# Keys instead of queries projected, narrow matmuls placed side by side in the array, and the attention ordered pair by pair

## The chip, the cores and the metric

The kernel runs on one core of a Trainium2 chip, alone, in one launch. The metric is the device time of the launch in microseconds (us), the median of several executions. Inside a launch five engines work from their own queues, strictly in the order in which the program lists their instructions: PE (TensorE, matrix products into the eight PSUM banks), DVE (VectorE), ACT (ScalarE), POOL (GpSimd) and SP, which here only issues DMAs. They wait for each other through semaphores.

## The reference

The input is 32 batches of 64 tokens with 128 features, so 2048 tokens in all. Each batch attends to its own 64 context tokens with 8 heads. Then comes a layer norm, a small feed-forward net (FFN) of width 256, a second layer norm, and a mixture of experts: two shared experts that every token uses and 16 routed ones, of which each token uses four, chosen by a router.

```python
def attention_block(query, ctx):              # query = layernorm(x), (32, 64, 128)
    q = einsum('bsd,hdk->bhsk', query, Wq)    # 8 heads of 128
    k = einsum('btd,hdk->bhtk', ctx, Wk)
    v = einsum('btd,hdv->bhtv', ctx, Wv)
    A = softmax(m * (q @ k^T) + (1 - m) * -1e30)
    proj = concat_heads(A @ v) @ Wo
    x1 = layernorm(ctx + proj) * gamma[0] + beta[0]
    ffn = relu(x1 @ W1 + b1) @ W2 + b2
    return layernorm(x1 + ffn) * gamma[1] + beta[1]
x = x + attention_block(layernorm(x), ctx)
h = layernorm(x)
scores = sigmoid(h @ router_w.T)              # 2 of 4 groups, then 4 of 16 experts
y = sum over experts e of combine[t, e] * ((silu(h @ gate[e]) * (h @ up[e])) @ down[e])
out = x + y + shared experts
```

## The kernel before

**Tiling.** The 2048 tokens are 16 tiles of 128 (`NT`). A tile is a pair of batches of 64 tokens. Four pairs make a chunk of 512 tokens (`CH = 4`, `TPC = 4`, `CW = 512`). A pair is written (c, p) for chunk and place before, and m = 0 to 15 after.

**Preparation.** On load the weights of a head are folded: PE transposes Wq, Wk and Wv (L1201, 24 transposes), multiplies Wq Wk^T (L1208) and Wv Wo (L1218), and ACT and DVE split each result in a high and a low part of type fp32r (`fold_high`, `fold_low`).

**Attention, by chunk.** PE transposes the normalised x and the context (`turn_xn`, `turn_ctx`). `queries` makes for every head the folded query of the whole chunk, as three fp32r matmuls of 512 columns (L1059 to L1061), and ACT copies each out of PSUM (L501). For a pair, `scores` runs eight fp32 matmuls of 128 columns (L1122); in each, half the result belongs to the other batch of the pair and is thrown away. `values` makes context times folded Wv Wo, six fp32r matmuls, and ACT copies them out (L510). The softmax of a pair goes over four engines: DVE adds the mask (L768, two instructions) and takes the maximum (L774), POOL subtracts it (L348), ACT takes the exponential (L516), DVE sums and inverts (L780, L783), POOL scales (L357). PE transposes the result (L1132), ACT spreads it into a block-diagonal tile (L525, two copies), `attend` runs eight fp32 matmuls of 128 columns over the heads into one bank (L1144), and DVE adds the context (L788).

**After attention, by chunk, one or two chunks behind:** layer norms (`statistics` and `normalise` on DVE, the inverse root on POOL as L338 or L343, L340), the FFN on PE (`turn_x1` L1159, `ffn_up` L1164, `ffn_down` L1171; `hidden` L535 on ACT), the turned and split input of the experts (`turn_xm` L1183, `xm_high`, `mT_low`) and the router's logits (`route`). The routing itself is about 40 small DVE instructions for eight tiles at a time (`bias_scores`, `group_scores`, `keep_groups`, `keep_experts`, `combine`).

**Experts.** A step k is one expert on one chunk: `up` (six fp32r matmuls, L1059 to L1061), silu on ACT (L646), the product on DVE (`gate_up`, L988 or L992), the routing weight (`weigh`, on POOL L447 in the first 16 steps, on DVE L1004 later), and `down` (one fp32 matmul of 512 columns, L1331). Before `up(0, k)` may write its second bank, `gate_up` of step k - 2 must be done. There are 72 steps. The first 16 are interleaved by hand with what is left of attention, FFN and routing of the last chunk; from step 16 on it is a steady loop.

**What sets the order** is on every engine an explicit list, in the loops `for c in range(CH + 1)` and in the hand-written sequences behind them (PE from L1334, DVE from L1008, ACT from L671, POOL from L456). PSUM is eight banks: three work banks in rotation, two for scores, and one each for transposed probabilities, attention result and FFN.

## Time and profile before

| what | value |
|---|---|
| median of three runs | 341.67 us (341.66 to 342.0) |
| profiled execution, its own time | 341.1 us |
| its span in the trace | 339.4 us |
| PE busy | 314.8 us, 93% |
| DVE busy | 220.9 us, 65% |
| ACT busy | 145.5 us, 43% |
| POOL busy | 92.0 us, 27% |
| attention, first query matmul to last attend | 15.4 to 152.1 us |
| first expert steps among the rest of the last chunk | 148.7 to 191 us |
| steady expert loop and output | 191 to 339.4 us |

The span is what the trace covers, 1.7 us less than the profiled execution's own time. Busy time of PE is summed over instructions whose ends are modelled, so the distance from the start of one instruction to the start of the next is the better price of one, and such distances are used below. An instruction marked x16 stands for sixteen that are merged in one row; every fp32 matmul is two PE instructions, and an fp32r matmul or a transpose is one.

### The profile page before, as it was taken

What the parts mean: (1) busy time and instruction counts of PE and PEld (TensorE: products, weight loads), DVE (VectorE), ACT (ScalarE), POOL (GpSimd) and SP (SyncE); (2) the same over time, 40 slices, a digit from 0 to 9 for tenths busy, and PEclk for the clock granted to TensorE, in tenths of its full rate; (3) what the DMA queues carried; (4) which work ended last, traced back from release to release, by engine and by line L of the source; (5) the groups of instructions that cost most, each with busy time, mean ns of one, the idle gap of its engine ahead of it and who ended that gap; (6) DMA issues with size and microseconds to landing.
All of it is one profiled execution on the core that took longest, in us unless ns stands there. A gap on an engine that the chain in (4) does not pass through costs nothing.

```text
span 339.4 us, 5140 instructions
## 1 busy us (share of the span) xinstructions
PE 314.8 (93%) x1611; PEld 240.6 (71%) x1611; DVE 220.9 (65%) x568; ACT 145.5 (43%) x266; POOL 92.0 (27%) x105
## 2 busy tenths in 40 slices
PE   3989899999999998986977999999999999999993
PEld 3979789788978896874655666666666666666662
DVE  2818526948895789798676835566566656565654
ACT  2664673477347734662325342333333233333320
POOL 3006413634473444453263042000000000000000
PEclk9999999999999999999997999999999999999999
DMA  8996000000000000002100046333233333323004
GB/s 243 349 272 214 3 0 3 0 0 2 1 3 0 2 0 2 0 4 74 57 0 1 2 138 240 124 116 106 95 118 124 124 124 124 122 114 102 32 0 124
DMA packets 18773, 26.79 MB, mean 79 GB/s; under 512 B 1330, under 2 KB 13124, under 8 KB 18628
## 3 DMA queue, kind: packets, MB, share of 16 engines
q1 hardware_dynamic: 16676, 25.52, 22.8%
q10 hardware_dynamic: 2080, 1.05, 1.1%
q8 instruction: 10, 0.16, 0.2%
q14 instruction: 7, 0.06, 0.0%
HBM read 25.38 MB, written 1.18 MB: 78 GB/s over the span
## 4 chain that ended last, share of the span: by engine, by line
PE 76%; DVE 12%; ACT 4%; issue 3%; POOL 2%; DMA 1%; DVEq 0%; POOLq 0%; ACTq 0%
PE bank L1331 17%; PE bank L1059 12%; PE bank L1061 12%; PE bank L1060 12%; PE bank L1144 8%; PE bank L1122 7%; DVE cen L725 3%; PE bank L1171 2%; DVE sc_m L768 2%; ACT prob_T L525 2%; PE bank L1201 1%; DMA wqk_in<-in_L_xattn_Wq 1%; ACT v_o L510 1%; DVE stat L709 1%; ACT hid L535 1%
## 5 line engine op out<-in xcount | busy, mean ns | idle before, releaser
L646 ACT ACTIVATE wT<-bank 128x512 f32<-128x512 f32 x72 | 43.0, 597 | 84.9 <-PE bank L1061 84.8
L1059 PE MATMUL bank<-mT_hi,we_hi 128*128 128x512 f32 x128 | 74.0, 578 | 3.9 <-DVE wT L992 2.0
L992 DVE TENSOR_TENSOR wT<-bank,wT 128x512 f32<-128x512 f32 x64 | 44.1, 691 | 39.5 <-PE bank L1061 29.8
L1061 PE MATMUL bank<-mT_hi,we_lo 128*128 128x512 f32 x128 | 50.5, 394 | 0.0
L1060 PE MATMUL bank<-mT_lo,we_hi 128*128 128x512 f32 x128 | 50.3, 393 | 0.0
L1059 PEld LDWEIGHTS bank<-mT_hi,we_hi 128*128 128x128 f32 x128 | 24.0, 188 | 22.0 <-issue 12.3
L398 POOL TENSOR_TENSOR we_lo<-w_exp,we_hi 128x256 fp32r<-128x256 f32 x16 | 11.8, 740 | 97.8 <-ACT we_hi L567 97.8
L1331 PE MATMUL bank<-wT,we_dn 128*128 128x512 f32 x72 | 37.5, 605 | 0.0
L1331 PE MATMUL bank<-q_T,we_dn 128*128 128x512 f32 x72 | 36.5, 592 | 0.0
L1060 PEld LDWEIGHTS bank<-mT_lo,we_hi 128*128 128x128 f32 x128 | 24.1, 188 | 16.7 <-issue 14.0
L1122 PEld LDWEIGHTS bank<-cT_m,q_T 128*128 128x128 f32 x256 | 30.3, 192 | 6.4 <-DVE sc_m L768 5.9
L1122 PE MATMUL bank<-cT_m,q_T 128*128 128x128 f32 x256 | 31.6, 276 | 3.2 <-DVE sc_m L768 3.2
L1144 PE MATMUL bank<-v_o,prob_T 128*128 128x128 f32 x256 | 31.9, 278 | 2.1 <-ACT prob_T L525 1.8
L1144 PEld LDWEIGHTS bank<-v_o,prob_T 128*128 128x128 f32 x256 | 30.1, 192 | 4.8 <-ACT prob_T L525 4.6
L1061 PEld LDWEIGHTS bank<-mT_hi,we_lo 128*128 128x128 f32 x128 | 24.0, 188 | 5.4
L348 POOL TENSOR_TENSOR sc_m<-sc_m,nmax 128x512 f32<-128x512 f32 x16 | 16.7, 1043 | 30.8 <-DVE nmax L774 30.8
L510 ACT COPY v_o<-bank 128x512 f32<-128x512 f32 x32 | 17.7, 588 | 15.9 <-PE bank L1144 9.1
L357 POOL TENSOR_TENSOR prob<-sc_m,rsum 128x512 f32<-128x512 f32 x16 | 16.7, 1043 | 25.9 <-DVE rsum L783 25.9
L525 ACT COPY prob_T<-bank 64x512 f32<-64x512 f32 x32 | 18.6, 580 | 7.7 <-PE bank L1132 7.5
L501 ACT COPY q_T<-bank 128x512 f32<-128x512 f32 x32 | 18.2, 589 | 7.7 <-PE bank L1061 5.9
L768 DVE TENSOR_TENSOR sc_m<-bank,mask_add 128x256 f32<-128x256 f32 x32 | 12.0, 416 | 10.3 <-PE bank L1122 10.3
L1331 PEld LDWEIGHTS bank<-q_T,we_dn 128*128 128x128 f32 x72 | 13.7, 190 | 4.3 <-issue 1.4
(181 smaller groups left out, 529.9 us busy)
## 6 DMA issues: line engine op xcount, KB each, us to landing
wvo_in<-comb_dram SPq DMA_DIRECT2D x16, 512.0 KB, 3.5
wqk_in<-comb_dram SPq DMA_DIRECT2D x15, 512.0 KB, 3.6
mask_row<-in_mask_BxS_ff SPq DMA_DIRECT2D x1, 1024.0 KB, 8.8
out_x<-ctx_all SPq DMA_DIRECT2D x4, 256.0 KB, 2.8
x_all<-in_x SPq DMA_DIRECT2D x1, 768.0 KB, 8.2
ctx_all<-in_ctx SPq DMA_DIRECT2D x1, 768.0 KB, 10.5
wqk_in<-in_L_xattn_Wq ACTq DMA_DIRECT2D x1, 512.0 KB, 4.8
wqk_in<-in_L_xattn_Wk ACTq DMA_DIRECT2D x1, 512.0 KB, 5.6
```

The lines of the kernel that those rows point to most:

```text
L501: a.copy(q_T[:, :, h, :], work[k % 3][:].rearrange("p (b s) -> p b s", s=SEQ)).then_inc(work_free[k % 3], 1)
L510: a.copy(v_o[p % 2][:, j * HP:(j + 1) * HP, :].rearrange("p h d -> p (h d)"), work[k % 3][:]).then_inc(work_free[k % 3], 1)
L525: last = a.copy(prob_T[p % 2][rows, :, s, :], t_bank[rows, :].rearrange("p (h s) -> p h s", s=SEQ))
L646: a.activation(silu[k % 2], h_bank[k % 2][:], ACT.Silu).then_inc(silu_ready, 1)
L768: last = v.tensor_tensor(sc_m[i][:, s], sc_bank[s][:].rearrange("p (h t) -> p h t", t=P)[:, :, 0:SEQ], mask_add[:, (2 * p + s) * SEQ:(2 * ...
L992: v.tensor_tensor(s_u[k % 2], u_bank[k % 2][:], silu[k % 2], ALU.mult).then_inc(s_u_ready, 1)
L1059: pe.matmul(dst, w_hi, m_hi, start=start, stop=False)
L1060: pe.matmul(dst, w_hi, m_lo, start=False, stop=False)
L1061: return pe.matmul(dst, w_lo, m_hi, start=False, stop=stop)
L1122: last = pe.matmul(sc_bank[s][:, hp * P:(hp + 1) * P], q_T[:, b, 2 * hp:2 * hp + 2, :].rearrange("p h s -> p (h s)"), cT_m[:, b * SEQ:b * ...
L1144: last = pe.matmul(av_bank[:, 0:P], prob_T[p % 2][:, h, :, :].rearrange("p b s -> p (b s)"), v_o[p % 2][:, h, :], start=(h == 0), stop=(h ...
L1331: pe.matmul(acc[c][:], we_dn[i][:], act[k % 4], start=start, stop=stop).then_inc(down_full, 1)
```

## The change

It rewrites the attention part, and the order of all that stands beside it.

- **Preparation.** The host lays out all weights and inputs as the kernel wants them (`layout`). Wq and Wk come transposed, so the 24 transposes fall away; the fold gives per head a matrix for keys. Only that one is split in high and low; the folded Wv Wo stays one fp32 tile `vo`. Loads are fewer and contiguous. A second copy of the context with its two halves swapped, `ctx_swap`, is loaded as well (1 MB), and the mask is brought in a form for pairs.
- **Keys projected.** `key(c, h)` takes the place of `queries`: the (masked) context of a chunk times the folded weight, three fp32r matmuls per head, copied out by ACT. It runs one chunk ahead: two heads per pair. The odd heads use the scores' bank.
- **Scores in column tiles.** A pair's scores are two fp32 matmuls of 512 columns with a stationary operand of 64 columns: one batch writes partitions 0 to 63 of the bank, the other 64 to 127. The mask is one DVE instruction.
- **Raw context attended in row tiles.** `values` is gone. `attend` multiplies the probabilities (one ACT copy in place of two) with the unprojected context: four fp32 matmuls of 256 columns whose contraction has 64 rows, in the upper or the lower half of the array, into two banks. `heads_out` copies both to SBUF on ACT, and `project` applies `vo`: eight fp32 matmuls of 128 columns.
- **Order.** One loop over m = 0 to 17 on every engine. Scores of pair m, and transposing, attending and projecting of pair m - 2, stand in one turn of it.
- **Beside it.** The layer norms 1 and 3 are applied by ACT in place of DVE (POOL makes one more small product for it). The routing of the first eight tiles stands behind the loop, among the first expert steps, in place of inside the last chunk. In the sequence behind the loop, `add_ctx` of the last pair follows `keep_groups(0)`, and `gate_up(0, 5)` follows `residual(3)` and `statistics(3, 3)`.

The core of the diff. PE:

```diff
-                    for hp in range(HP):
-                        last = pe.matmul(sc_bank[s][:, hp * P:(hp + 1) * P],
-                                         q_T[:, b, 2 * hp:2 * hp + 2, :].rearrange("p h s -> p (h s)"),
-                                         cT_m[:, b * SEQ:b * SEQ + P], start=True, stop=True)
+                    tok = n * P + s * SEQ
+                    pe.matmul(sc_bank[s * SEQ:(s + 1) * SEQ, :], xnT[:, tok:tok + SEQ],
+                              k_T[c % 2][:, b, :, :].rearrange("p h t -> p (h t)"), start=True, stop=True
+                              ).then_inc(sc_full, 1)
...
+            def attend(n):
+
+                pe.wait_ge(prob_T_ready, n + 1)
...
+                for s in range(2):
+                    for j in range(2):
+                        rows = slice(j * SEQ, (j + 1) * SEQ)
+                        held = ctx_all if s == j else ctx_swap
+                        last = pe.matmul(o_bank[j][:].rearrange("p (h b s) -> p h b s", b=2, s=SEQ)[:, :, s, :],
+                                         held[rows, n, :], prob_T[n % 2][rows, :, s, :], start=True, stop=True)
+                        if s == 1:
+                            last.then_inc(o_full[j], 1)
+
+            def project(n):
+
                 for j in range(2):
...
+                    pe.wait_ge(o_taken[j], n + 1)
...
                 for h in range(NH):
...
+                    last = pe.matmul(av_bank[:, 0:P], o_T[n % 2][:, h % 2, h // 2, :], vo[:, h, :],
+                                     start=(h == 0), stop=(h == NH - 1))
...
+            for m in range(NT + 2):
+                c, p = divmod(m, TPC)
+                ahead = c + 1 < CH
+                if m < NT:
+                    scores(m)
+                if ahead:
+                    key(c + 1, 2 * p)
+                if m >= 2:
+                    turn_probs(m - 2)
...
+                if p == 0 and c >= 2:
+                    ffn_up(c - 2, 1)
+                if p == 0 and c >= 3:
+                    turn_xm(c - 3)
+                if p == 1 and c >= 2:
+                    ffn_down(c - 2)
...
+                if m >= 2:
+                    attend(m - 2)
+                if ahead:
+                    key(c + 1, 2 * p + 1)
...
+                if p == 3 and c + 2 < CH:
+                    turn_ctx(c + 2)
+                if p == 3 and c >= 1:
+                    ffn_up(c - 1, 0)
+                if m == NT + 1:
+                    pe.wait_ge(sc_taken, NT)
+                    up(0, 0)
+                if m >= 2:
+                    project(m - 2)
```

ACT:

```diff
+                if ahead:
+                    key(c + 1, 2 * p)
+                if m >= 2:
+                    spread(m - 2)
...
+                if p == 0 and c >= 2:
+                    hidden(c - 2, 1)
+                if p == 0 and c >= 3:
+                    xm_high(c - 3)
...
+                if m < NT:
+                    exponent(m)
+                if m >= 2:
+                    heads_out(m - 2)
+                if ahead:
+                    key(c + 1, 2 * p + 1)
+                if m == NT:
                     router_sigmoid(0)
```

DVE:

```diff
+            for m in range(NT + 1):
+                c, p = divmod(m, TPC)
+                if m >= 3:
+                    add_ctx(m - 3)
+                if m >= 1:
+                    sum_of_exp(m - 1)
+                if m < NT:
+                    mask_and_max(m)
+                if c == 0 and p + 1 < CH:
+                    if p == 0:
+                        v.wait_ge(ld_x, 16)
+                    statistics(0, p + 1, tokens(x_all, p + 1))
+                    normalise(0, p + 1, tokens(x_all, p + 1))
+                if m == 0:
+                    cT_low(1)
...
+            add_ctx(NT - 2)
+            bias_scores(0)
+            group_scores(0)
+            add_ffn(CH - 2)
+            statistics(2, CH - 2, z)
+            keep_groups(0)
             gate_up(0, 0)
...
+            add_ctx(NT - 1)
+            v.wait_ge(y_ready, NT)
+            statistics(1, CH - 1, tokens(y, CH - 1))
+            residual(CH - 2)
             gate_up(0, 1)
+            keep_experts(0)
             statistics(3, CH - 2, tokens(x2, CH - 2))
             gate_up(0, 2)
...
+            combine(0)
             gate_up(0, 3)
+            take_combine(0)
             add_ffn(CH - 1)
             statistics(2, CH - 1, z)
             gate_up(0, 4)
-            gate_up(0, 5)
             residual(CH - 1)
             statistics(3, CH - 1, tokens(x2, CH - 1))
+            gate_up(0, 5)
```

POOL, the opening, the loop and the sequence behind it:

```diff
+            mask_context(0)
             inverse_root(0, 0)
...
+            mask_context(1)
+            pool.wait_ge(ld_mask, 32)
+            pool.tensor_scalar(mask_add[:], mask_add[:], -1.0, BIG, ALU.add, ALU.mult).then_inc(mask_done, 1)
...
+            for m in range(NT + 1):
+                c, p = divmod(m, TPC)
+                if m >= 1:
+                    normalise_probs(m - 1)
+                if m < NT:
+                    subtract_max(m)
+                if c == 0 and p + 1 < CH:
+                    inverse_root(0, p + 1)
...
+            inverse_root(2, CH - 1)
             weigh(4)
-            inverse_root(2, CH - 1)
             weigh(5)
             mT_low(CH - 2)
             inverse_root(3, CH - 1)
```

## Rows read from the trace of the kernel before

**Rows 1.** The page: PE busy in 40 slices, and the clock granted to it.

```profile
PE   3989899999999998986977999999999999999993
PEclk9999999999999999999997999999999999999999
```

**Rows 2.** Timeline, PE, opening: start us, us, engine, line, operation, out<-in, merged count.

```profile
5.71 3.65 PE L1201 MATMUL bank<-ident,wqk_in 128*128 128x128 f32 x16 [5.71 <-DMA wqk_in<-in_L_xattn_Wq]
16.23 0.39 PE L1059 MATMUL bank<-xnT_hi,qk_hi 128*128 128x512 f32 x1
16.91 0.39 PE L1059 MATMUL bank<-xnT_hi,qk_hi 128*128 128x512 f32 x1
22.36 1.95 PE L1122 MATMUL bank<-cT_m,q_T 128*128 128x128 f32 x16
```

**Rows 3.** Timeline, PE, one pair: scores, attend, four transposes, and what follows.

```profile
32.03 1.95 PE L1122 MATMUL bank<-cT_m,q_T 128*128 128x128 f32 x16
33.82 1.95 PE L1144 MATMUL bank<-v_o,prob_T 128*128 128x128 f32 x16
35.61 0.60 PE L1132 MATMUL bank<-ident,prob 128*128 128x128 f32 x4
35.96 0.48 PE L1059 MATMUL bank<-vo_hi,cT_hi 128*128 128x512 f32 x1
```

**Rows 4.** Timeline, PE: scores of the first pair of chunks 1 and 3.

```profile
52.05 1.95 PE L1122 MATMUL bank<-cT_m,q_T 128*128 128x128 f32 x16
120.34 1.95 PE L1122 MATMUL bank<-cT_m,q_T 128*128 128x128 f32 x16
```

**Rows 5.** DMA issues: size and us from issue to landing.

```profile
wvo_in<-in_L_xattn_Wo SPq DMA_DIRECT2D x1, 512.0 KB, 7.2
ctx_all<-in_ctx SPq DMA_DIRECT2D x1, 768.0 KB, 10.5
```

**Rows 6.** Timeline: the softmax of the first pair through DVE, POOL and ACT.

```profile
24.34 0.76 DVE L768 TENSOR_TENSOR sc_m<-bank,mask_add 128x256 f32<-128x256 f32 x2 [7.04 <-PE bank L1122]
25.96 1.04 POOL L348 TENSOR_TENSOR sc_m<-sc_m,nmax 128x512 f32<-128x512 f32 x1 [5.81 <-DVE nmax L774]
27.04 0.63 ACT L516 ACTIVATE sc_m<-sc_m 128x512 f32<-128x512 f32 x1 [3.90 <-POOL sc_m L348]
28.63 0.68 DVE L780 TENSOR_REDUCE esum<-sc_m 128x8 f32<-128x512 f32 x1
29.46 0.83 DVE L709 BATCH_NORM_STATS2 stat<-x_all 128x6 f32<-128x128 f32 x4
```

**Rows 7.** Timeline, ACT in chunk 3: an exponential, the next instruction, a pair of copies.

```profile
129.00 0.63 ACT L516 ACTIVATE sc_m<-sc_m 128x512 f32<-128x512 f32 x1 [0.20 <-POOL sc_m L348]
129.54 0.29 ACT L561 ACTIVATE wqk_in<-logits 128x128 f32<-128x128 f32 x1
143.65 1.07 ACT L510 COPY v_o<-bank 128x512 f32<-128x512 f32 x2 [1.49 <-PE bank L1144]
```

**Rows 8.** Timeline: an fp32 matmul of 512 columns, and its reader's start.

```profile
160.68 1.02 PE L1164 MATMUL bank<-x_T,w_in 128*128 128x512 f32 x2
161.74 0.69 ACT L535 ACTIVATE hid<-bank,small_T 128x512 f32<-128x512 f32 x1 [0.96 <-PE bank L1164]
```

**Rows 9.** Windows with the routing's tile alone on DVE: busy us and count.

```profile
129.80:150.80 21.00, 9.22 (x43) 1.00 0.01 2
```

**Rows 10.** Timeline behind the attention: from the last pair to expert step 9.

```profile
153.85 0.29 DVE L788 TENSOR_TENSOR ctx_all<-bank,ctx_all 128x128 f32<-128x128 f32 x1
166.81 0.69 DVE L793 TENSOR_TENSOR x_b<-bank,x_b 128x512 f32<-128x512 f32 x1 [2.27 <-PE bank L1171]
169.71 1.29 POOL L447 TENSOR_TENSOR wT<-wT,wqk_in 128x512 f32<-128x512 f32 x1 [6.62 <-DVE wT L992]
181.07 1.09 PE L1183 MATMUL bank<-ident,cen 128*128 128x128 f32 x4 [1.72 <-DVE cen L725]
184.72 0.47 PE L1059 MATMUL bank<-mT_hi,we_hi 128*128 128x512 f32 x1
```

More of the change, by code:

```diff
@@ L518, in spread @@
-            def spread(c, p):
-                a.wait_ge(t_full, c * TPC + (p + 1))
-                if not (c == 0 and p < 2):
-                    a.wait_ge(av_full, c * TPC + (p - 1))
-                for s in range(2):
-                    rows = slice(s * SEQ, (s + 1) * SEQ)
-                    last = a.copy(prob_T[p % 2][rows, :, s, :],
-                                  t_bank[rows, :].rearrange("p (h s) -> p h s", s=SEQ))
-                last.then_inc(prob_T_ready, 1)
+                    for h in range(NH - 2, NH):
+                        a.wait_ge(key_full[h % 2], key_use(c - 1, h))
@@ L913, in take_combine @@
                 v.tensor_copy(comb_T[0:rows, b, :], comb_bank[b][0:rows, 0:P]).then_inc(comb_T_ready, 1)
-            for c in range(CH + 1):
-                now, last, before = c < CH, c >= 1, c >= 2
-                if last:
-                    sum_of_exp(c - 1, 3)
-                if before:
+            for m in range(NT + 1):
[14 more added lines that the diff above has]
+                if p == 0 and c >= 3:
+                    mT_low(c - 3)
+                    take_logits(c - 3)
+                if p == 1 and c >= 2:
@@ L921, in _ @@
                     add_ffn(c - 2)
[L922 to L925 removed]
                     statistics(2, c - 2, z)
[L927 to L935 removed]
+                if p == 2 and c >= 1:
@@ L976, in _ @@
-                add_ctx(c, 1)
-                if c + 1 == CH:
-                    keep_experts(0)
+                if p == 3 and c + 2 < CH:
+                    cT_low(c + 2)
             def gate_up(j, k):
@@ new lines, in _ @@
+                        a, b = (1, 0) if i == 0 else (0, 1)
+                        last = pe.matmul(fold_bank[2 * i + half][:, h * P:(h + 1) * P], w_in[:, i, half, h, a, :],
+                                         w_in[:, i, half, h, b, :], start=True, stop=True)
+                    last.then_inc(fold_done, 1)
+                if i == 0:
+                    turn_ctx(0)
+                    turn_xn(0)
+            pe.wait_ge(fold_lo, 2)
+            for h in range(NH):
+                key(0, h)
```

840 lines of the change are left out of this document (344 added, 496 removed).

## The prediction

> **What bounds the kernel now.** I began with the page's 40 slices: PE is at 9 tenths nearly everywhere, with a dip where attention hands over to the experts, and its clock is granted in full except near that dip [rows 1]. So PE's order is what to read, and I read its timeline next. One pair of the attention shows the prices. Eight fp32 matmuls of 128 columns take 1.79 us from start to start, as scores (33.82 - 32.03) and as attend (35.61 - 33.82); four transposes take 0.35 [rows 3]. An fp32r matmul of 512 columns takes a third of 16.91 - 16.23, that is 0.227 [rows 2]. A pair of before is then 1.79 scores, 1.79 attend, 0.35 transposes, twelve fp32r matmuls (queries and values) 2.72: 6.65 us. FFN, router and the turning of inputs bring it to what the trace has: from chunk 1 to chunk 3 (120.34 - 52.05) / 8 = 8.54 us [rows 4]. Nearly all of it is PE at work, since softmax, copies and norms of other pairs lie beside it. The steady expert loop, from 191 us, is the same in both kernels and keeps its length. What the change can move is the opening, 16 pairs, and the stretch up to expert step 9, which starts at 184.72 [rows 10].
>
> **PE's work per pair after.** Keys cost what queries cost, 1.36. Values (1.36) and attend (1.79) go; the new attend and project (1.79) come. The attend has 4 x 256 columns, as many as eight of 128: 1.79 one behind another. The new scores have 2 x 512 columns, again 1.79 one behind another. No row shows two matmuls side by side in the array, so both have open prices. Upper end: nothing overlaps, 1.79 each, and PE's sum is 1.36 + 1.79 + 0.35 + 1.79 + 1.79 = 7.08, 0.43 more than before. Lower end: two always run together, 0.90 each, 5.30. Below that nothing, since each half of the array still has its columns to stream. I take the middle. Each fp32 matmul is two instructions on the same half of the array. If instructions start in order, the first of a matmul stands alone, and only the second has the other half's first beside it: three slots of four, 0.45 each. Attend then takes five slots of eight, 1.12. PE's sum is 1.36 + 1.34 + 0.35 + 1.12 + 1.79 = 5.96.
>
> The Trainium skill, TensorE: Matmul & The Clock Gate (Part 3: Packing small matmuls), has matmuls in different tiles run at once, started and ended in program order, and gives 2.38x for three column tiles; with a plain 2x the scores would stand at the lower end. No trace here shows it. TensorEngine Tiling (Array Packing) in the Trainium skill (Key Properties) speaks against the change: a change of tiling mode, not merely of tile, drains the engine. That would come four times per pair; nothing in these rows shows such a change.
>
> **Which wait ends last in a turn.** PE is in order, and project(m - 2) stands ahead of scores(m + 1). It waits for heads_out(m - 2), which on ACT is queued behind exponent(m), which needs scores(m). So each turn holds a closed ring:
> - Scores until DVE starts: one fp32 matmul of 512 columns until its reader takes 161.74 - 160.68 = 1.06 [rows 8]; a third slot adds 0.45: 1.51 (1.06 to 1.96 at the ends).
> - Mask add to exponential: 27.04 - 24.34 = 2.70, through maximum and POOL's subtraction [rows 6]; one mask instruction in place of two saves about 0.1: 2.60.
> - Exponential to ACT's next: 129.54 - 129.00 = 0.54; heads_out is two copies, 1.07 [rows 7]; to PE about 0.05.
> - Project 1.79 [rows 3].
> Sum 7.56 us, with PE busy 5.96 of it. The ring is longer than PE's work. Spread, attend and key copies lie inside it: from the end of the scores' slots, key 0.68 and turning 0.35, spread about 0.8 with its wait, attend 1.12, and the last copy reach project at some 4.0, against 4.4 by the ring. With attend at 1.79 they reach it at 4.5. Even full overlap of scores wins little, for DVE has its own list: add_ctx(m - 3), which needs project, then the sum of m - 1, 29.46 - 28.63 = 0.83 [rows 6], and only then the mask: some 0.2 + 0.3 + 0.83 = 1.35 behind the start of scores. The ring can't fall under 7.4.
>
> FFN work stands inside the turns. What the ring doesn't cover: ffn_up (0.90) with turn_ctx (0.35) behind the odd key in turn 7, 0.6; ffn_down ahead of attend in turn 9, 0.3; hidden and xm_high ahead of exponent(12) on ACT, 1.2; the others 0.2 together. 2.3 in all, 0 to 4.7 for other overlaps of attend.
>
> **The opening.** Before, the transposes start at 5.71 when the first weights land, and the first scores at 22.36 [rows 2]. After, folding starts at about 5.7; its second weight pair is the 2.5th MB, as Wo was (issued at 3.6, landed 7.2 later) [rows 5]: 10.8 plus 0.9 of folding, keys of chunk 0 from 11.6, eight times 0.68, turn_ctx(1): scores(0) at 17.6, 4.8 earlier. But the mask needs POOL: context of the other chunks (issued at 8.2 before and landed 10.5 later [rows 5], behind 5.0 MB; now behind 4.0, I take 15), 1.1 of masking, and 1024 mask elements, which I put at 3.1: DVE starts at 19.3. Key(1, 0) waits for DVE's cT_low(1), queued behind maximum, statistics and normalise with a POOL root in between: 25.2; scores(1) at 27.4. Scores(2) comes at 32.7; turn 2 has one more round of norms ahead of its mask, scores(3) at 41.2, scores(4) at 48.8, where before had 52.05 [rows 4]: 3.3 us ahead. Faster contiguous loads could give 2 more; a late vector load would cost 1.
>
> **The loop.** 12 turns of 7.56 and 2.3: turn 16 starts at 48.8 + 90.7 + 2.3 = 141.8. A pair gains 0.8 us over 8.54.
>
> **The hand-over.** It takes this back. The pipe is two pairs deep, so turns 16 and 17 have only turning, attend and project, and wait on ACT: turn 16 about 6.0, turn 17 (0.35 + ffn_down 1.79 + attend 1.12 + up 1.36 + project 1.79) 6.4: the last project ends at 154.3. Before, its DVE reader began at 153.85 [rows 10]. Now DVE has the routing's 9.2 us of work [rows 9] here, no longer inside chunk 3; half of it and an FFN addition with statistics stand ahead of add_ctx(15), which comes at 156, and turn_combine(0) holds PE once more, to 166.7. ffn_down(3) ends at 170.9; before, its reader began at 166.81 [rows 10]: 4.1 later. From there before needed 14.3 us to turn_xm(3) at 181.07, partly because POOL's weigh(4), 1.29, stood ahead of a root [rows 10]; moving that root ahead gives 1.3, and norms on ACT, beside DVE's list in place of in it, by my estimate 1.5. But gate_up(0, 5) now follows statistics(3, 3), so POOL's weigh(5) and mT_low, 1.3 each, end up ahead of the last root: 2.6 lost, less 0.4 of overlap. turn_xm(3) comes at 184.6, and step 9 at 186.8, against 184.72 [rows 10]: +2.1. The steps behind it keep their pace. The output goes out in larger pieces: -0.3. A change between narrow and full matmuls may cost PE a pause: an attached reader sees a fp32 matmul end 1.06 after its start though it takes 0.90 of PE's time [rows 3, 8], so up to 0.16 for each of 16 returns to scores, 0 to 2.6; I take 1.3.
>
> **The sum.** 341.1 + 2.1 - 0.3 + 1.3 = 344.2 for an execution like the profiled one. The median of the runs lies 0.6 above that execution, so 344.8.
>
> **The rivals.**
> - No overlap in the array: that the change doesn't do what it says. Ring 8.01, so 0.45 x 14 = 6.3 more, 2.4 for FFN work, 1.3 in the last two attends: 354.8. For it speaks that no row shows overlap. Decided by whether the scores' instructions start 0.45 us apart or together. Chance 0.17.
> - The ring doesn't bind, PE's work does: 5.96 and 1.1 of other work is 7.1 for eight turns, 5.7 for four without keys: turn 16 at 128, 13 less: 331. Decided where exponential and copies leave project free less than 4.0 us after the scores' slots. For it: before, PE waited little for the same softmax. Against: there exponent(c, p) stood ahead of no copy that the next scores wait for. Chance 0.20.
> - The clock falls: before, one slice behind the dip was granted 0.7 of full [rows 1], after waits of PE. The turns of chunk 3 and the hand-over keep PE busy only 60%; 8 us of work at half clock (1.2 in place of 2.4 GHz) cost 4 to 8 more, I take 4: 349. This is the case that ends slower by one place, turns 12 to 17, from the point at which PE's waits there are as long as at that dip. Chance 0.08.
> - Two scores at once, the skill's rule worked out: the ring is bound by DVE's list at 1.43 in place of 1.51, 1.3 less: 343.5. The section on packing named above states that rule of the Trainium skill. Chance 0.05.
>
> **How the numbers follow.** 0.2% (0.7 us) is about what a measurement of this kernel can tell from no change. The forecast has 0.50, with 339 to 350 from the opening (2), FFN cover (2.3) and pauses (1.3): 0.10 faster, 0.05 the same, 0.35 slower. With the rivals: faster 0.10 + 0.20 + 0.02 = 0.32, same 0.07, slower 0.61. The range holds the no-overlap case up to 355 and reaches to 335, leaving out much of the second rival.
>
> **What would show it.** Right: turns of 7.5 us in the trace, PE waiting ahead of project for ACT's copies, scores(4) near 49, PE waiting for DVE between 155 and 167, turn_xm(3) near 185. Wrong: turns near 7.1 (PE's work binds) or 8.0 (no overlap); a first scores(1) far from 27; a POOL or DVE list that runs late in every turn.

## The result, and the profile after

The changed kernel takes 353.81 us (median; 352.09 to 354.17), the one before 341.75 beside it: a ratio of 1.034, 95% interval 1.031 to 1.038. It is 12.1 us slower where 3.1 was forecast. The sign was right and the time lies inside the range; the size was not right. The profiled execution took 354.17 us with a span of 352.4; the forecast for it was 344.2, so 10.0 us have to be found. An execution that takes over 1.5% more than the fastest of its kernel counts in no median or ratio here (one of e11_tail).

The page's slices (8.8 us each) answer [rows 1].

```profile
PE   2783979889998986899595999999999999999995
...
PEclk9997699999999999899898799999999999999999
```

The steady expert loop in the right half is as full as before. The fourth slice (26 to 35 us), where attention opens, has PE at 3 tenths and starts a stretch whose clock falls to 0.6; the 20th and 22nd, in the hand-over to the experts, have PE at 5 tenths. The same in stretches (us, busy time and count of PE, PE's weight loads, DVE, ACT, POOL, then the granted clock):

```profile
20.00:45.00 25.00, 17.36 (x62) 9.47 (x62) 12.09 (x39) 9.35 (x17) 9.10 (x12) 0.80 0.52 177
...
114.00:150.00 36.00, 29.73 (x188) 21.11 (x188) 20.51 (x67) 19.17 (x39) 19.80 (x22) 0.95 0.00 1
150.00:200.00 50.00, 41.60 (x214) 31.06 (x213) 30.42 (x126) 24.51 (x47) 19.49 (x21) 0.90 0.07 23
```

The opening, which answers [rows 2, 6]. First what held PE and DVE ahead of the keys (PE, then DVE):

```profile
13.23 1.11 PE L1026 MATMUL bank<-ident,cen 128*128 128x128 f32 x4 [1.82 <-DVE cen L736]
14.14 3.16 PE L1156 MATMUL bank<-w_in 128*128 128x128 f32 x16
17.06 0.48 PE L1016 MATMUL bank<-cT_hi,qk_hi 128*128 128x512 f32 x1
```

```profile
9.44 0.87 DVE L716 BATCH_NORM_STATS2 stat<-x_all 128x6 f32<-128x128 f32 x4 [9.44 <-DMA x_all<-in_x]
```

Then from the first scores to the second:

```profile
24.41 1.08 PE L1063 MATMUL bank<-k_T,xnT 128*64 128x512 f32 x4
25.53 0.69 DVE L762 TENSOR_TENSOR sc_m<-bank,mask_add 128x512 f32<-128x512 f32 x1 [10.56 <-PE bank L1063]
...
29.50 1.11 DVE L736 TENSOR_SCALAR cen<-x_all,mean_var,rstd 128x128 f32<-128x128 f32 x4 [1.16 <-POOL rstd L335]
30.53 0.68 DVE L753 TENSOR_TENSOR cT_lo<-bank,cT_hi 128x512 fp32r<-128x512 f32 x1
...
31.27 0.80 PE L1016 MATMUL bank<-cT_hi,qk_hi 128*128 128x512 f32 x1 [5.78 <-DVE cT_lo L753]
...
34.87 1.97 PE L1063 MATMUL bank<-k_T,xnT 128*64 128x512 f32 x4 [0.68 <-ACT k_T L509]
```

Line by line: chunk 0 of x lands at 9.44; its norm keeps turning (L1026), and with it the second fold (L1156 at 14.14), waiting, so keys start at 17.06 and not at 11.6. That fold takes 3.16 us behind PE's wait of 1.82, where sixteen such products take 1.95 at the full clock (experiments below). Scores(0) come at 24.41. Then PE waits 5.78 us until DVE has worked through maximum, statistics, a POOL root and the norm to cT_low(1). After that wait its records stretch: the same scores take 1.97 in place of 1.08 us, which is the 1.2 GHz level in place of 2.4.

One turn of the loop, which answers [rows 3, 4, 6]: timeline of all engines from one scores to the next.

```profile
64.55 1.08 PE L1063 MATMUL bank<-k_T,xnT 128*64 128x512 f32 x4
...
65.77 0.69 DVE L762 TENSOR_TENSOR sc_m<-bank,mask_add 128x512 f32<-128x512 f32 x1
...
67.68 0.48 PE L1086 MATMUL bank<-prob_T,ctx_all 64*128 64x256 f32 x1 [0.73 <-ACT prob_T L544]
67.69 0.48 PE L1086 MATMUL bank<-prob_T,ctx_swap 64*128 64x256 f32 x1
...
68.33 0.63 ACT L536 ACTIVATE sc_m<-sc_m 128x512 f32<-128x512 f32 x1 [0.71 <-POOL sc_m L352]
...
68.90 1.07 ACT L531 COPY o_T<-bank 128x512 f32<-128x512 f32 x2
...
70.07 2.02 PE L1098 MATMUL bank<-vo,o_T 128*128 128x128 f32 x16 [0.37 <-issue]
...
72.03 0.65 PE L1063 MATMUL bank<-k_T,xnT 128*64 128x512 f32 x2
```

(The last row counts two of the four instructions of scores, for the view ends there.) The ring can be read off: scores to mask 1.22, mask to exponential 2.56, exponential to copies 0.57, copies until project 1.17, project 1.96. The sum is 7.48, where 7.56 was forecast. The eleven turns from scores(4) at 57.07 to scores(15) at 143.41 take 86.3 us. One of them, turn 14, takes 8.80, because its project ran at the lower clock behind a wait of 2.00:

```profile
140.09 3.39 PE L1098 MATMUL bank<-vo,o_T 128*128 128x128 f32 x16 [2.00 <-ACT o_T L531]
```

From 134 to 150 us the granted clock is 0.89; in e1_ct below it is 1.00 there, and turn 14 takes 7.44. So 1.4 us of the 86.3 are the clock's.

The hand-over answers [rows 10]:

```profile
170.71 1.11 PE L1111 MATMUL bank<-ident,cen 128*128 128x128 f32 x4 [3.25 <-ACT cen L517]
...
176.72 0.27 PE L1175 MATMUL bank<-ident,comb_w 128*128 128x128 f32 x1
...
179.08 1.95 PE L1123 MATMUL bank<-w_in,hid 128*128 128x128 f32 x16
```

```profile
189.90 1.28 POOL L452 TENSOR_TENSOR k_T<-prob,w_in 128x512 f32<-128x512 f32 x1 [3.84 <-DVE prob L940]
...
191.13 1.27 POOL L458 TENSOR_TENSOR mT_lo<-xm_T,mT_hi 128x512 fp32r<-128x512 f32 x1
...
192.35 1.04 POOL L337 TENSOR_TENSOR rstd<-var_eps,neg_half 128x4 f32<-128x4 f32 x1
```

POOL's weigh(5) (L452) and mT_low (L458) do stand ahead of the last root (L337), as forecast; turn_combine (L1175) shows no wait, which was not forecast. turn_xm(3) comes at 195.50 and step 9 at 198.65. From there to the end of the span the changed kernel takes 0.9 us less than the one before: 352.4 - 198.65 = 153.75, and 339.4 - 184.72 = 154.68.

### The profile page after: what moved, and what is told of

It is laid out like the page before. It is cut to its first block, busy times and chain, and to the rows that moved or that the text cites. A ratio compares the mean times of both kernels' runs of the same rounds, so it can differ in the third digit from the quotient of the medians.

```text
span 352.4 us, 4746 instructions
## 1 busy us (share of the span) xinstructions
PE 310.4 (88%) x1426; PEld 212.8 (60%) x1426; DVE 192.9 (55%) x511; ACT 145.0 (41%) x278; POOL 97.7 (28%) x114
## 3 DMA queue, kind: packets, MB, share of 16 engines
q10 hardware_dynamic: 288, 1.05, 1.0%
## 4 chain that ended last, share of the span: by engine, by line
PE 75%; DVE 10%; issue 4%; POOL 4%; ACT 4%; DMA 2%; SPq 0%; DVEq 0%; POOLq 0%; ACTq 0%
PE bank L1219 17%; PE bank L1016 12%; PE bank L1018 11%; PE bank L1017 11%; PE bank L1098 9%; PE bank L1063 4%; PE bank L1086 3%; DMA x_all<-in_x 2%; PE bank L1116 2%; DVE stat L716 2%; PE bank L1123 2%; DVE cen L736 1%; ACT prob_T L544 1%; ACT o_T L531 1%; POOL sc_m L352 1%
## 5 line engine op out<-in xcount | busy, mean ns | idle before, releaser
L647 ACT ACTIVATE sc_m<-bank 128x512 f32<-128x512 f32 x72 | 43.0, 597 | 82.4 <-PE bank L1018 78.8
L1219 PE MATMUL bank<-k_T,we_dn 128*128 128x512 f32 x144 | 73.4, 596 | 0.0
L1098 PE MATMUL bank<-vo,o_T 128*128 128x128 f32 x256 | 33.5, 286 | 8.8 <-ACT o_T L531 6.3
L1098 PEld LDWEIGHTS bank<-vo,o_T 128*128 128x128 f32 x256 | 31.4, 199 | 14.6 <-ACT o_T L531 13.5
L509 ACT COPY k_T<-bank 128x512 f32<-128x512 f32 x32 | 18.9, 592 | 42.3 <-PE bank L1018 41.7
L940 DVE TENSOR_TENSOR sc_m<-bank,sc_m 128x512 f32<-128x512 f32 x32 | 22.1, 690 | 22.2 <-PE bank L1018 13.7
L1219 PEld LDWEIGHTS bank<-k_T,we_dn 128*128 128x128 f32 x144 | 27.3, 192 | 8.3 <-issue 2.7
L940 DVE TENSOR_TENSOR prob<-bank,sc_m 128x512 f32<-128x512 f32 x32 | 22.1, 690 | 16.8 <-PE bank L1018 14.4
L952 DVE TENSOR_TENSOR k_T<-sc_m,w_in 128x512 f32<-128x512 f32 x28 | 19.8, 708 | 8.9 <-PE bank L1219 5.7
L952 DVE TENSOR_TENSOR k_T<-prob,w_in 128x512 f32<-128x512 f32 x28 | 19.4, 693 | 5.7 <-PE bank L1219 5.5
L337 POOL TENSOR_TENSOR rstd<-var_eps,neg_half 128x4 f32<-128x4 f32 x12 | 12.7, 1056 | 26.5 <-DVE var_eps L725 26.5
```

The costliest lines, as they stand in the source:

```text
L509: a.copy(k_T[c % 2][:, :, h, :], key_bank[i][:].rearrange("p (b s) -> p b s", s=SEQ)).then_inc(key_free[i], 1)
L647: a.activation(silu[k % 2], h_bank[k % 2][:], ACT.Silu).then_inc(silu_ready, 1)
L940: v.tensor_tensor(s_u[k % 2], u_bank[k % 2][:], silu[k % 2], ALU.mult).then_inc(s_u_ready, 1)
L952: v.tensor_tensor(act[k % 4], s_u[k % 2], comb[i][:, c * CW:(c + 1) * CW], ALU.mult).then_inc(weighed_ready, 1)
L1098: last = pe.matmul(av_bank[:, 0:P], o_T[n % 2][:, h % 2, h // 2, :], vo[:, h, :], start=(h == 0), stop=(h == NH - 1))
L1219: pe.matmul(acc[c][:], we_dn[i][:], act[k % 4], start=start, stop=stop).then_inc(down_full, 1)
```

## The experiments

Each is an edit of the changed kernel or of another experiment, timed beside the kernel before. They stand by the part of the forecast that they are about: the opening, the turn, the overlap inside the array, the hand-over.

**The opening.** cT_low(1) on DVE directly behind the mask of pair 0:

```diff
                 if m < NT:
                     mask_and_max(m)
+                if m == 0:
+                    cT_low(1)
                 if c == 0 and p + 1 < CH:
...
                     normalise(0, p + 1, tokens(x_all, p + 1))
-                if m == 0:
-                    cT_low(1)
```

> DVE takes cT_low(1) directly behind mask_and_max(0), ahead of the statistics and norm of chunk 1. Theory A (the opening was mis-sized: key(1, 0) stands on PE behind a DVE list, PE idles 5.8 us and then works at a lower granted clock until 50 us): key(1, 0) starts near 27.5 in place of 31.3, the second scores near 30 in place of 34.9, and the clock stays full; 5 to 6 us less, about 348 us. Theory B (the ring of a turn is longer than I took it, or the bulk of the loss is in the hand-over): under 1 us less, since the loop from scores(4) on would take the time up.

349.75 us (349.27 to 351.02), ratio 1.0245 (1.0217 to 1.0273): 4.1 less than the changed kernel. Scores(1) start at 31.70 and scores(4) at 52.99, against 34.87 and 57.07; by the medians the 4.1 us won in the opening arrive at the end in full. So one DVE instruction at the wrong place in the list is about a third of the loss. Less was won than the 5 to 6 us expected: key(1, 0) starts at 28.18, 3.1 earlier, and the granted clock from 20 to 45 us rises from 0.80 to 0.93, not to full.

Another delay in the opening, x's norm ahead of the second fold; here the fold and the keys go first, on PE, ACT and DVE (the parts of PE and DVE):

```diff
                     turn_ctx(0)
-                    turn_xn(0)
             pe.wait_ge(fold_lo, 2)
...
                 key(0, h)
+            turn_xn(0)
             turn_ctx(1)
...
-            v.wait_ge(ld_x0, 16)
-            statistics(0, 0, tokens(x_all, 0))
-            normalise(0, 0, tokens(x_all, 0))
             for i in range(2):
...
             cT_low(0)
+            v.wait_ge(ld_x0, 16)
+            statistics(0, 0, tokens(x_all, 0))
+            normalise(0, 0, tokens(x_all, 0))
```

> The second fold and the keys of chunk 0 go ahead of turn_xn(0) on PE and ACT, and DVE splits the fold and the context ahead of the norm of chunk 0. Theory A1 (late landing of x, 9.4 us, delays everything): scores(0) starts near 20.8 in place of 24.4 and the kernel gains about 3 us. Theory A2 (behind scores(0) POOL waits for the vector load until 26.1 before it may subtract the first maximum, and cT_low(1) hangs behind POOL's root on DVE): scores(0) moves by 3.6 but the second scores by under 0.7 us, and the time is within 1 us of 353.8.

352.87 us (350.32 to 353.21), ratio 1.0304 (1.0257 to 1.035): 0.9 less by the medians, which these spreads don't separate from nothing. PE's timeline:

```profile
13.19 1.16 PE L1156 MATMUL bank<-w_in 128*128 128x128 f32 x8 [0.59 <-DMA w_in<-in_w_attn]
14.10 0.48 PE L1016 MATMUL bank<-cT_hi,qk_hi 128*128 128x512 f32 x1
...
29.69 0.79 PE L1016 MATMUL bank<-cT_hi,qk_hi 128*128 128x512 f32 x1 [6.56 <-DVE cT_lo L753]
```

Keys start 3.0 us earlier, scores(0) 2.4, but the wait for cT_low(1) grows to 6.56 and scores(4) come only 1.6 earlier (55.49). The last weights are used at 13.19, as they land: even with the right order the keys can't start at 11.6. POOL's timeline shows why so little arrives:

```profile
25.00 0.61 POOL L405 TENSOR_SCALAR b_beta<-vec_row 128x128 f32<-128x128 f32 x1 [4.22 <-DMA vec_row<-in_vec]
25.70 1.04 POOL L352 TENSOR_TENSOR sc_m<-sc_m,nmax 128x512 f32<-128x512 f32 x1
```

The maximum was taken at 23.90 in 0.69 us, but POOL's list has the small vector's use ahead of the subtraction, and the vector lands only now; the root that cT_low(1) waits for comes behind both. In the changed kernel the vector's use starts at 26.06 and the subtraction at 27.09, right behind a maximum that is done at 26.95: late keys and a late vector are nearly equal bounds there. So A2's cause is in the trace, though scores(1) moved by 1.6 and not by under 0.7.

Nor is all of the 3.0 us the order's. e3_ring, e5_g5 and e7_both below leave this part as it is, yet their keys start at 15.27 to 15.37. The rows of e5_g5:

```profile
13.59 1.95 PE L1156 MATMUL bank<-w_in 128*128 128x128 f32 x16
15.30 0.48 PE L1016 MATMUL bank<-cT_hi,qk_hi 128*128 128x512 f32 x1
```

Against 3.16 and 17.06 in the changed kernel's profile, some 1.7 us of the keys' lateness is the lower clock in this fold, and 1.2 is the order. With keys this early, scores(1) still come at 33.09 to 34.54, and the vector's use at 24.76 to 26.39.

**The turn.** On ACT, heads_out and the odd key's copy ahead of the exponential, which opens the forecast's ring:

```diff
-                if m < NT:
-                    exponent(m)
                 if m >= 2:
                     heads_out(m - 2)
                 if ahead:
                     key(c + 1, 2 * p + 1)
+                if m < NT:
+                    exponent(m)
```

> On ACT, heads_out(m - 2) and the odd key's copy go ahead of exponent(m). If the ring scores, mask, maximum, subtraction, exponential, heads_out, project sets the turn (7.5 to 7.6 us between scores in the trace), the ring opens and turns fall to PE's own work with its waits for spread and heads_out, 6.4 to 6.9 us: 12 turns x 0.8 is 8 to 12 us less, about 344. If PE's own order sets the turn, it stays at 7.5 and the time within 1 us of 353.8.

349.43 us (348.22 to 351.57), ratio 1.0226 (1.0175 to 1.0277): 4.4 less, where 8 to 12 were expected. Turns with keys and without FFN work still take 7.49 (scores at 62.98 and 70.47). Turns that fall: turn 2 from 8.41 to 7.54, turn 12 from 7.92 to 7.40, turn 14 to 6.69 (from 7.44 without the clock's part), and turn 15 up to its project by 0.8; 2.9 in all. The rest of the 4.4 isn't traced to the edit. The timeline of a turn with keys names the second chain:

```profile
65.00 0.58 ACT L509 COPY k_T<-bank 128x512 f32<-128x512 f32 x1 [3.06 <-PE bank L1018]
65.48 0.59 ACT L544 COPY prob_T<-bank 128x512 f32<-128x512 f32 x1
...
66.13 0.48 PE L1086 MATMUL bank<-prob_T,ctx_all 64*128 64x256 f32 x1 [0.73 <-ACT prob_T L544]
...
67.35 1.07 ACT L531 COPY o_T<-bank 128x512 f32<-128x512 f32 x2 [1.27 <-PE bank L1086]
...
68.52 2.02 PE L1098 MATMUL bank<-vo,o_T 128*128 128x128 f32 x16 [0.37 <-issue]
```

ACT no longer stands between exponential and copies (it waits 1.27 for the attend), and project still starts 68.52 - 62.98 = 5.54 behind the scores; in the changed kernel it is 70.07 - 64.55 = 5.52. The chain scores, key, turning of the probabilities, its copy behind the key's, attend, copies is as long as the ring.

That second chain shortened alone: probabilities turned ahead of the even key, on PE and on ACT.

```diff
-                if ahead:
-                    key(c + 1, 2 * p)
                 if m >= 2:
                     turn_probs(m - 2)
+                if ahead:
+                    key(c + 1, 2 * p)
...
-                if ahead:
-                    key(c + 1, 2 * p)
                 if m >= 2:
                     spread(m - 2)
+                if ahead:
+                    key(c + 1, 2 * p)
```

> The transposes of pair m - 2 go ahead of the even key on PE, and spread ahead of its copy on ACT. Theory A (two chains of nearly equal length bind each turn: scores to exponential to heads_out, and turn_probs to spread to attend to heads_out): the second gets shorter by about 0.8 us but the first still holds project, so turns stay near 7.4 and the gain is under 1.5 us in all. Rival (only the second chain binds): turns fall to about 6.7 and the kernel gains 6 to 9 us.

353.4 us (351.11 to 354.12), ratio 1.0315 (1.0278 to 1.0352): nothing gained beyond the spread, as expected for two chains; turns 4 to 6 take 7.43. Both edits together:

> e3_ring and e6_turn together. Theory A (two chains): turns fall to 6.5 to 6.8 us with keys and about 6.4 without, so some 10 to 12 us less than the kernel after, 342 to 345. If PE's own order or switching between narrow and full matmuls sets the turn: 7.4 as before, about 349.

344.65 us (342.51 to 347.54, ten runs), ratio 1.0096 (1.0065 to 1.0127): 9.2 less, where the parts alone gave 4.4 and 0.4. PE's rows of two scores:

```profile
60.21 1.08 PE L1063 MATMUL bank<-k_T,xnT 128*64 128x512 f32 x4
...
66.90 0.65 PE L1063 MATMUL bank<-k_T,xnT 128*64 128x512 f32 x2
```

The turn is 6.69 us: turns 4, 5, 6 and 10. Two chains of nearly equal length bound it, and each edit alone left the other one in place. Turns with FFN work gain less: 7 to 9 take 7.76, 7.49 and 8.42, for 8.18, 7.56 and 8.46 in the changed kernel. The eight turns of chunks 1 and 2 average 7.22 in place of 7.74.

**The overlap.** Scores at full width, one batch's matmul behind the other (the first batch's scores of each pair are written over, so left out of the result):

```diff
-                    tok = n * P + s * SEQ
-                    pe.matmul(sc_bank[s * SEQ:(s + 1) * SEQ, :], xnT[:, tok:tok + SEQ],
+                    pe.matmul(sc_bank[:], xnT[:, n * P:(n + 1) * P],
```

> The two score matmuls of a pair take the whole stationary tile of 128 columns and the whole bank, so they can't run beside each other; the second overwrites the first, so the scores of the first batch of each pair are left out. Scores then take 1.8 in place of 1.01 us of PE per pair. If full overlap was hidden by DVE's own list (mask add 1.2 us behind the start of the scores whatever their length), the turn grows by the part beyond it, about 0.45 to 0.7 us for 14 turns, and the kernel by 6 to 9 us: 360 to 363. If PE has slack in the turn beyond that, under 2 us.

364.32 us (363.2 to 365.92), ratio 1.0675 (1.0637 to 1.0713): 10.5 more than the changed kernel, where 6 to 9 were expected. PE's rows of both kernels, the scores and the first two matmuls of the key behind them; first the wide one:

```profile
60.32 1.88 PE L1062 MATMUL bank<-k_T,xnT 128*128 128x512 f32 x4
61.64 0.79 PE L1016 MATMUL bank<-cT_hi,qk_hi 128*128 128x512 f32 x1
62.27 0.39 PE L1017 MATMUL bank<-cT_lo,qk_hi 128*128 128x512 f32 x1
...
66.56 2.02 PE L1097 MATMUL bank<-vo,o_T 128*128 128x128 f32 x16 [0.49 <-issue]
68.42 1.02 PE L1062 MATMUL bank<-k_T,xnT 128*128 128x512 f32 x2
```

The changed kernel:

```profile
79.52 1.08 PE L1063 MATMUL bank<-k_T,xnT 128*64 128x512 f32 x4
80.53 0.50 PE L1016 MATMUL bank<-cT_hi,qk_hi 128*128 128x512 f32 x1
80.87 0.40 PE L1017 MATMUL bank<-cT_lo,qk_hi 128*128 128x512 f32 x1
```

Four instructions of the narrow scores have 1.01 us until the key starts. One full-width fp32 matmul of that size needs 0.90 of PE's time by [rows 3], so two narrow ones run side by side in full, and some 0.1 remains. The key's second matmul starts 1.35 behind the scores, against 1.95 in the wide kernel: 0.60 a turn; the turn grows from 7.48 to 8.10 (60.32 to 68.42). The attend shows it too: its two inputs start at 67.68 and 67.69, and the eight instructions have 1.06 us until the next matmul.

**The hand-over.** DVE's gate_up(0, 5) ahead of residual(3) and statistics(3, 3), so that POOL's weigh(5) isn't ahead of the root:

```diff
             gate_up(0, 4)
+            gate_up(0, 5)
             residual(CH - 1)
             statistics(3, CH - 1, tokens(x2, CH - 1))
-            gate_up(0, 5)
```

> gate_up(0, 5) goes back ahead of residual(3) and statistics(3, 3) on DVE. Theory A (POOL's weigh(5) and mT_low(2), 1.28 and 1.27 us, stand ahead of the last inverse root because weigh(5) waits for gate_up(0, 5)): the root starts about 2 us earlier, turn_xm(3) near 193.5 in place of 195.5, and the kernel gains 1.5 to 2.2 us: about 352. Rival: PE's work or ACT's norms set that stretch, and nothing moves (within 0.5 us).

353.8 us (351.82 to 355.67), ratio 1.0367 (1.0318 to 1.0417): no difference that its spread lets one see. In its profile turn_xm(3) comes 32.8 us behind the start of project(15), against 33.6 in the changed kernel, so 0.8 of the 2.6 forecast for these two POOL instructions. Another 2.0 went lost on the way: now POOL's weigh(4), weigh(5) and mT_low follow each other from 182.68 to 186.45, and the norm on DVE beside them takes twice as long as in the changed kernel (2.08):

```profile
182.75 4.04 DVE L736 TENSOR_SCALAR cen<-x_b,mean_var,rstd_g 128x128 f32<-128x128 f32 x4 [0.34 <-POOL rstd_g L341]
```

Inconclusive in time.

The routing taken out of the hand-over (the router's choice for the first eight tiles is left out, with constant weights in its place):

```diff
-            bias_scores(0)
-            group_scores(0)
             add_ffn(CH - 2)
...
-            keep_groups(0)
...
-            keep_experts(0)
...
-            combine(0)
+            v.memset(comb_w[:, 0], 0.15).then_inc(route_done, 1)
```

> The kernel after without the routing of the first eight tiles in the hand-over: their routing weights are a constant, so those tokens get every expert with the same weight. In the prediction this routing cost the hand-over some 4 us (ffn_down(3) 4.1 us later, turn_combine(0) held). Theory A (the trace after): turn_combine(0) isn't held, add_ctx(15) comes only 1.1 us late, so 1 to 1.5 us less, 352.5. Rival (the prediction): 3 us or more, under 351.

351.98 us (350.88 to 353.19), ratio 1.0284 (1.0258 to 1.031): 1.8 less. turn_x1(3) stays at 170.64, ffn_down(3) moves from 179.08 to 177.65 and turn_xm(3) from 195.50 to 194.07. This run reached project(15) 0.7 later than the changed kernel, with a granted clock of 0.79 from 134 to 150 us; counted from project(15), both are 2.1 earlier. The routing costs 1.4 to 2.1 us here, not 3 or more.

**All together, and a faster kernel.** Both edits of the turn, both of the opening, gate_up(0, 5) early, and on SP the small vector loaded earlier:

```diff
+            sp.dma_start(vec_row[:], vec.partition_broadcast(P)).then_inc(ld_vec, 16)
             for now, ld in ((slice(0, TPC), ld_swap0), (slice(TPC, NT), ld_swap)):
...
-            sp.dma_start(vec_row[:], vec.partition_broadcast(P)).then_inc(ld_vec, 16)
             sp.dma_start(small_T[:], small).then_inc(ld_small, 16)
```

> All edits together: both chains of the turn, cT_low(1) early, keys ahead of turn_xn(0), the vector load ahead of the bulk of the context, and gate_up(0, 5) early. If the three causes (opening, turn, hand-over) add up: e7_both less 4 (early cT_low), less 2 to 4 (keys and vectors, now uncovered), less 1.5 to 2: 334 to 338, faster than the kernel before. If they hide each other: 341 or more.

337.3 us (336.5 to 339.09), ratio 0.9859 (0.9836 to 0.9881): faster than before. Scores(4) start at 48.83. That this is the forecast's own 48.8 is chance: the order is another. Then one turn in 6.7, without FFN work; turn_xm(3) at 179.21.

On top of it, keep_groups(0) moved behind add_ctx(15) and statistics(1, 3):

```diff
             statistics(2, CH - 2, z)
-            keep_groups(0)
             gate_up(0, 0)
...
             statistics(1, CH - 1, tokens(y, CH - 1))
+            keep_groups(0)
             residual(CH - 2)
```

> e8_all with keep_groups(0) on DVE behind add_ctx(15) and statistics(1, 3). There the last project ended at 148.3 and add_ctx(15) began at 149.6. Theory A (that DVE list is what makes the hand-over longer): everything up to step 9 starts 1.2 us earlier, 336. Rival: a later wait takes it up, within 0.5 us of 337.3.

340.41 us (338.27 to 342.85, ten runs), ratio 0.9948 (0.9925 to 0.9971): 3.1 more than without it, against both expectations. PE's timeline:

```profile
154.78 0.66 PE L1111 MATMUL bank<-ident,cen 128*128 128x128 f32 x4 [2.30 <-ACT cen L517]
...
163.44 0.33 PE L1175 MATMUL bank<-ident,comb_w 128*128 128x128 f32 x1 [1.44 <-DVE comb_w L887]
167.48 1.95 PE L1123 MATMUL bank<-w_in,hid 128*128 128x128 f32 x16
```

turn_x1(3) gains 0.6 (155.39 before the edit), but now turn_combine(0) waits for the routing and ffn_down(3) behind it comes 3.6 later (163.89 before the edit), part of it at half clock (0.79 granted from 155 to 163 us, 0.66 from 163 to 168). The wait that was forecast for the changed kernel shows here, once its cover is gone.

The other way out, on PE, with keep_groups(0) where it was: ffn_down(3) ahead of turn_combine(0).

```diff
             ffn_up(CH - 1, 1)
-            turn_combine(0)
             pe.wait_ge(y_ready, NT)
             down(0, 1)
-            up(0, 4)
             ffn_down(CH - 1)
+            turn_combine(0)
+            up(0, 4)
```

> e8_all with ffn_down(3) on PE ahead of turn_combine(0) and up(0, 4). The chain ffn_down(3), norm 2, norm 3, turn_xm(3) ends last in the hand-over, so ffn_down(3) 1.5 us earlier should bring turn_xm(3) 1.5 us forward: 335.5 to 336.3. Rival: gate_up(0, 4) then comes later on DVE and POOL's list (weigh(4), weigh(5), mT_low) keeps the last root where it is: 337.

335.02 us (334.49 to 335.64), ratio 0.9799 (0.9785 to 0.9814), the best of all: 6.9 us faster than the kernel before, and a little under the 335.5 to 336.3 expected. From turn_x1(3) to ffn_down(3) it takes 161.38 - 154.31 = 7.1 us, against 8.5. That is 1.4 of the 2.3 gained; another 1.1 is already there at turn_x1(3), where the opening's granted clock (20 to 45 us) was 1.00 and not 0.86, which the edit doesn't explain. (The profile of e8_all is of its slowest execution, 339.09 us, so the two profiles lie further apart than the medians.) Both moves together:

> e9_ctx and e10_ffn together on e8_all. If both edits act on one chain they add: 334.5 to 335.5. If they only fill each other's slack: 336 to 337.

335.58 us (333.54 to 337.49, five runs; a sixth took 339.65), ratio 0.9813 (0.9777 to 0.9849). No better than the last one alone, with intervals that overlap.

## Why the prediction was right and wrong

The sign was right, and the place of the loss was not. Against the kernel before, step 9 was forecast 2.1 us later: 3.3 won up to scores(4), 3.7 lost from there to the end of the last project, 1.6 lost behind it. Measured it is 13.9 later: 5.0 lost, 4.8 lost, 4.1 lost. (The three points: 52.05, 153.85 and 184.72 before; 48.8, 154.3 and 186.8 forecast; 57.07, 163.7 and 198.65 measured.) A gain forecast for the opening was a loss; that the sum still has the right sign is in part luck. The 10.0 us missing in the sum lie here.

- **The opening: the step that failed, 8.3 us.** It put scores(4) at 48.8; they came at 57.07. The lateness: 5.5 at the first key, 6.2 at the mask, 6.1 at key(1, 0), 7.5 at scores(1), 8.3 at scores(4). Three of its terms were wrong. First, the keys, at 17.06 and not 11.6: 2.5 because the last weight pair landed later than Wo had (with keys first they start at 14.10), and 3.0 in the fold behind turn_xn(0), of which some 1.7 is the lower clock; x lands at 9.44, third in its queue. The text had read the weight queue and not the order of the new PE list. Second, the small vector, to which the text gave 1 us: POOL starts its use at 26.06, so the subtraction, by the forecast due at some 20.7 (the mask at 19.3 and two DVE instructions), could not start before 26.7 even with keys at 11.6. The traces show this bound; no run moved the vector alone. Third, the clock: the keys of chunk 1 ran at half clock after PE's wait of 5.78, 3.6 us from key(1, 0) to scores(1) where 2.2 was forecast. The mask, forecast at 19.3 for POOL's sake, came at 25.53, right behind the scores; POOL was ready at 20.75, for two misses nearly cancelled: the context came at 18.57, not 15, and the mask instruction of 1024 elements took 1.05, not 3.1. The wait for cT_low(1) was forecast rightly (5.7 from mask to key(1, 0), 5.9 forecast), so it is in both sums, as a loss that the order makes and not as a miss of the forecast; by e1_ct it is worth 4.1.
- **PE's work per pair: the overlap was mis-sized, without effect.** Three slots of four were forecast, 1.34 for the scores; side by side in full it is 1.01. The Trainium skill, TensorE: Matmul & The Clock Gate (Part 3: Packing small matmuls), states this overlap, and the trace agrees. That DVE's list, not the scores, would then set the mask (1.35 forecast) was right: 1.22.
- **Which wait ends last in a turn: right in size, incomplete in cause.** 7.48 against 7.56, term by term within 0.3. But the second chain was put 0.4 shorter than the ring, and e3_ring with e6_turn show it equal. The rival in which PE's work binds (331) is refuted for this kernel; with both chains cut, in e7_both, eight turns of chunks 1 and 2 average 7.22, near the 7.1 of that rival.
- **The rival without overlap (354.8): its number came true, by accident.** Measured are 353.81. Its own test decides against it: the scores of a pair have 1.01 us of PE, not 1.79, and the turn is 7.48, not 8.01. e4_wide, which takes the overlap away, costs 10.5 more, and the rival had put 10.0 on that.
- **The loop and FFN cover: nearly right.** From 57.07 to the end of turn 15's project (148.89 + 1.79 = 150.7) it is 93.6, forecast 93.0. 1.4 of it is the clock in turn 14, so the work itself took 92.2.
- **The hand-over: direction right, 2.95 too small.** Behind the loop's 8.9 the lateness against the forecast is 9.4 at the last project's end (161.87 + 1.79 = 163.7 for 154.3), 10.0 at ffn_down(3)'s (180.87 for 170.9), 10.9 at turn_xm(3), 11.85 at step 9. It grows in small steps. The last of them, 0.95, is a slip of the sum: it left 2.2 us from turn_xm(3) to step 9, where before had 3.65 [rows 10], and gave no reason; measured are 3.15. The clock is in it too: from 190 to 200 us, behind waits of PE of 2.30 and 1.62, the granted clock is 0.66, but the kernel before, whose times the forecast used here, had 0.60 from 181 to 185. How much of the 2.95 the clock is was not measured apart. The step on routing failed in the other way: turn_combine(0) holds PE in no row of the changed kernel, since PE arrives late itself, and the routing costs 1.4 to 2.1 in all. The two POOL instructions ahead of the root were there, 1.3 each.
- **Pauses between narrow and full matmuls: 0.1 seen one way, nothing the other.** Project until scores takes 1.96, and 1.86 in the kernel with full-width scores (66.56 to 68.42 above): 0.10. The key's first matmul behind narrow scores has 0.34 until the next, but an expert's first behind the full-width project has 0.32 too, with no switch between:

```profile
163.57 0.48 PE L1016 MATMUL bank<-mT_hi,we_hi 128*128 128x512 f32 x1
163.89 0.39 PE L1017 MATMUL bank<-mT_lo,we_hi 128*128 128x512 f32 x1
```

  The Trainium skill, TensorEngine Tiling (Array Packing) (Key Properties), has a change of tiling mode drain the engine. No row here shows a drain as such; a pause of 0.10 us from full to narrow would fit it. It lies in project's 1.96 of the 7.48.
- **Output and steady loop:** from step 9 on 0.9 less than before, 0.3 forecast.

The ledger: 11.85 at step 9, less the 1.3 of pauses that the forecast had added in a term of its own, less 0.6 behind step 9, is 9.95 of the 10.0. The 0.6 for median over profiled run fell out the other way (353.81 against 354.17), so the median was missed by 9.0.

The rival of the falling clock had its mechanism right and its place too narrow: in turns 12 to 17, where it was looked for, it took 1.4 us in turn 14 (114 to 150 us has 0.95), and it was lowest between 20 and 45 us (0.80), where the forecast itself had put long waits of PE and had charged none of them.

## What to carry to other kernels

When a cycle of waits is found in a loop, work out the second-longest one with the same care: here two chains put project's start 5.52 and 5.54 us behind the scores, and only cutting both moved the turns with keys (9.2 us, where the parts gave 4.4 and 0.4). A reordering's cost lies where its pipeline is not yet full: write down the new issue order of each engine for the opening instruction by instruction, with the landing time of each operand in queue order, and move what the next engine waits for (here one 0.68 us cast worth 4.1 us) ahead of what only keeps the queue tidy. Where the forecast itself has PE wait, price the work behind that wait at both clocks: behind the waits of 5.8 to 7.2 us for cT_low(1) the lower one came in all eight profiles that have such a wait, behind waits of 1.7 to 2.1 us in some and not in others.

## What the runs showed of the hardware

- Two fp32 matmuls of 512 columns in two column tiles of 64 start together and have 1.01 us until the next matmul; a full-width one has 0.90. Attends in two row tiles of 64 overlap as fully: 1.06 for eight instructions of 256 columns.
- From full to narrow tiles a pause of about 0.1 us was seen; from narrow back to full none beyond what a first matmul behind a full one takes (0.34 and 0.32).
- Behind the same wait of 1.7 to 1.8 us in the opening, the second fold (sixteen products) took 1.95 us in three profiles and 2.86 to 3.62 in five: which clock follows a short wait varied from execution to execution.
- Executions of one kernel spread with the granted clock: e8_all took 339.09 us at a mean of 0.975 and 336.5 at 0.989. The kernel before, with 0.993 in its profile, spread from 341.02 to 342.29 beside it.
- A norm of four tiles on DVE (L736) took 1.11 us in the first two rounds of the opening, and 1.83 in the third, beside POOL's masking; in the hand-over, beside POOL's weigh, it took 2.08, and in e5_g5 and e8_all, with gate_up(0, 5) early and three POOL instructions in a row beside it, 4.04 and 4.03. In e10_ffn, where POOL's first multiply starts at 169.78, behind the end of the norm (167.90 + 1.11), it took 1.11. That POOL's instructions are the cause was not tried apart. DVE and POOL in the changed kernel:

```profile
184.76 1.30 POOL L452 TENSOR_TENSOR k_T<-sc_m,w_in 128x512 f32<-128x512 f32 x1
184.83 2.08 DVE L736 TENSOR_SCALAR cen<-x_b,mean_var,rstd_g 128x128 f32<-128x128 f32 x4 [0.94 <-POOL rstd_g L341]
```
